# Router softmax of a tile split in three steps, its exponentials and normalization placed behind the previous tile's residual

## The reference, cut to what matters

```python
nx = layer_norm(x)
evidence = softmax(nx @ Wq @ k.T / 16) @ v
combined = concatenate([nx, evidence, anchor])
router_probs = softmax(combined @ router_W + router_b)           # [tokens, 3]
h = silu(einsum(combined, e_w1) + e_b1)                          # 3 experts x 512
routed = sum((einsum(h, e_w2) + e_b2) * router_probs, experts)
g = sigmoid(silu(combined @ gate_w1 + gate_b1) @ gate_w2 + gate_b2)
x1 = x + g * (routed @ out_w + out_b)
# second layer, on x1
q = (ada_ln(x1) @ Wq + bq)      # 16 heads of 16
out = x1 + softmax(q @ k.T / 4) @ v @ Wp + bp
```

## Time and profile before

| | |
|---|---|
| time, median of 3 runs | 438.69 us (437.05 to 439.32) |
| the profiled execution: its own time | 439.1 us |
| its span, from the first to the last instruction | 437.3 us |
| TensorE's mean granted clock | 0.988 of full speed |
| busy share of the span | PE 97%, PEld 88%, DVE 68%, ACT 51%, POOL 42% |
| chain that ended last, by engine | PE 75%, DVE 15%, DMA 3%, issue 3%, ACT 2% |

### The profile page before, as it was taken

The page is one execution under the profiler, slowest core; times in us unless marked ns, Lnnn a source line. Parts: engine busy times, 40 slices in busy tenths (PEclk is TensorE's granted clock), DMA queues, the critical chain, the costliest instruction groups (busy, mean ns, idle before and its releaser), DMA issues.

```text
span 437.3 us, 9617 instructions
## 1 busy us (share of the span) xinstructions
PE 422.5 (97%) x3613; PEld 383.6 (88%) x3613; DVE 297.5 (68%) x748; ACT 223.9 (51%) x487; POOL 185.1 (42%) x192
## 2 busy tenths in 40 slices
PE   7999999999999999999999999999999899979995
PEld 6578999999998899989998899889988897868875
DVE  2685475683776497739963897389558865982696
ACT  2777643345347633863467246724763466317271
POOL 3545573553453346323633454346343732341020
PEclk9699999999999999999999999999999999998999
DMA  9678001640200221024000400030003021200301
GB/s 285 229 269 323 23 28 31 164 96 19 56 4 2 55 67 28 25 56 138 1 5 13 109 1 5 16 84 0 5 22 77 0 54 35 73 4 25 72 3 49
DMA packets 16982, 27.94 MB, mean 64 GB/s; under 512 B 3816, under 2 KB 9256, under 8 KB 16808
## 3 DMA queue, kind: packets, MB, share of 16 engines
q1 hardware_dynamic: 16808, 27.32, 21.4%
q10 hardware_dynamic: 128, 0.01, 0.0%
HBM read 16.07 MB, written 2.10 MB: 42 GB/s over the span
## 4 chain that ended last, share of the span: by engine, by line
PE 75%; DVE 15%; DMA 3%; issue 3%; ACT 2%; SPq 1%; ACTq 0%
PE hidden_banks L1704 7%; PE hidden_banks L1705 7%; PE hidden_banks L1706 7%; PE score_banks L1711 5%; PE score_banks L2076 5%; PE token_bank L1704 5%; PE token_bank L1705 5%; PE token_bank L1706 5%; PE score_banks L2046 4%; PE value_bank L2099 3%; PE value_bank L2102 3%; PE value_bank L1711 3%; DVE head_maxima L1468 3%; PE hidden_banks L1929 2%; DMA unit_weights<-units 2%
## 5 line engine op out<-in xcount | busy, mean ns | idle before, releaser
L1627 POOL TENSOR_TENSOR hidden_low<-hidden,hidden_high 128x512 fp32r<-128x512 f32 x56 | 72.8, 1300 | 113.7 <-ACT hidden_high L1075 113.6
L1468 DVE TENSOR_REDUCE head_maxima<-score_banks 128x2 f32<-128x308 f32 x128 | 54.6, 474 | 16.6 <-PE score_banks L2046 14.4
L1704 PE MATMUL hidden_banks<-normed_high,hidden_w_high 128*128 128x256 f32 x224 | 64.2, 287 | 0.8 <-issue 0.8
L1705 PE MATMUL hidden_banks<-normed_high,hidden_w_low 128*128 128x256 f32 x224 | 62.5, 279 | 0.0
L1706 PE MATMUL hidden_banks<-normed_low,hidden_w_high 128*128 128x256 f32 x224 | 62.4, 279 | 0.0
L1137 ACT ACTIVATE exp_ring<-score_banks 128x512 f32<-128x512 f32 x96 | 52.6, 600 | 18.8 <-PE score_banks L2076 17.8
L1075 ACT CAST hidden_high<-hidden 128x512 fp32r<-128x512 f32 x56 | 34.9, 622 | 47.8 <-DVE hidden L1385 46.8
L1704 PE MATMUL token_bank<-expert_out_high,hidden_high 128*128 128x256 f32 x192 | 55.6, 289 | 0.0
L1067 ACT ACTIVATE hidden<-hidden_banks 128x512 f32<-128x512 f32 x56 | 33.4, 596 | 40.4 <-PE hidden_banks L1929 38.8
L1706 PE MATMUL token_bank<-expert_out_low,hidden_high 128*128 128x256 f32 x192 | 53.4, 278 | 0.0
L1705 PE MATMUL token_bank<-expert_out_high,hidden_low 128*128 128x256 f32 x192 | 53.4, 278 | 0.0
(11 more groups left out here) (289 smaller groups left out, 1119.7 us busy)
## 6 DMA issues: line engine op xcount, KB each, us to landing
unit_weights<-units SPq DMA_DIRECT2D x7, 768.0 KB, 6.4
query_stack<-queries_high SPq DMA_DIRECT2D x56, 64.0 KB, 2.0
tokens<-x SPq DMA_DIRECT2D x8, 256.0 KB, 3.8
query_stack<-queries_low SPq DMA_DIRECT2D x28, 64.0 KB, 2.0
w_slice<-units SPq DMA_DIRECT2D x7, 256.0 KB, 2.9
out<-tokens SPq DMA_DIRECT2D x7, 256.0 KB, 2.4
w_T<-folds SPq DMA_DIRECT2D x6, 256.0 KB, 6.1
pair_keys<-keys_high SPq DMA_DIRECT2D x16, 77.0 KB
```

What stands on the lines that cost most here:

```text
L1468: v.tensor_reduce(MX[:, s, first:first + step + 1:step], S[:, ring_of[key][0], 0:2 * CTX].rearrange("p (j n) -> p j n", j=2), AX.X, ALU.ma ...
L1627: nc.gpsimd.tensor_tensor(SL[:, ring(t, u), :], TB[:, ring(t, u), :], raw(SH[:, ring(t, u), :]), ALU.subtract).then_inc(gpsimd_h, 1)
L1704: mm(out_, lh, rh, start=start, stop=False, skip_group_check=skip)
L1705: mm(out_, ll, rh, start=False, stop=False, skip_group_check=skip)
```

## The change

The step `logit` is cut in three. `logit` keeps the two additions. `top` is the maximum, on DVE. `soft` is the two exponentials on ACT, and the reciprocal and the two scalings on DVE. Each has a slot of its own: `top` at 17, just ahead of `res` of the tile before (17.4); `soft` at 18.6, behind `shift` (18.5), with -0.8 on ACT where the exponentials had +1.7 to a slot of 14.4. Tile 0 is placed by the table of the setup. No instruction is added or dropped and none changes its operands; line numbers grow by 2 to 10.

```diff
-    "ln": 0.2, "norm": 1.6, "low": 6.6, "att": 7.9, "prob": 9.1, "route": 12.3, "logit": 14.4, "res": 17.4,
+    "ln": 0.2, "norm": 1.6, "low": 6.6, "att": 7.9, "prob": 9.1, "route": 12.3, "logit": 14.4, "top": 17, "soft": 18.6, "res": 17.4,
...
-        "logit": 1.7, "z": 0.81, "h": 0.3, "gate": 0.4, "qx": 0.4, "query": 0.1, "row": -0.4, "score": 0.2,
+        "soft": -0.8, "z": 0.81, "h": 0.3, "gate": 0.4, "qx": 0.4, "query": 0.1, "row": -0.4, "score": 0.2,
...
                 v.tensor_tensor(LG[:, :, :], LG[:, :, :], parts_of[:, 0, :, 0:EXPERTS], ALU.add).then_inc(vector_logit, 1)
-                dve.wait_ge(vector_logit, upto(vector_logit, key, "l"))
-                v.tensor_reduce(RT[:, 0, :], LG[:, :, :], AX.X, ALU.max, negate=True).then_inc(vector_logit, 1)
-                dve.wait_ge(scalar_logit, upto(scalar_logit, key, "ex"))
+
+            def top(key):
+                t = key[1]
+                dve.wait_ge(vector_logit, upto(vector_logit, ("logit", t), "l"))
+                if t:
+                    dve.wait_ge(scalar_soft, upto(scalar_soft, ("soft", t - 1), "ex"))
+                v.tensor_reduce(RT[:, 0, :], LG[:, :, :], AX.X, ALU.max, negate=True).then_inc(vector_top, 1)
+
+            def soft(key):
+                t = key[1]
+                dve.wait_ge(scalar_soft, upto(scalar_soft, key, "ex"))
                 v.reciprocal(RT[:, 2, :], RT[:, 1, :]).then_inc(vector_results, results.one())
                 dve.wait_ge(vector_results, results.n)
                 for s in range(NSUB):
                     last = v.tensor_scalar(PR[:, t % 2, s, :], PR[:, t % 2, s, :], RT[:, 2, s:s + 1], None, ALU.mult)
-                last.then_inc(vector_logit, 1)
+                last.then_inc(vector_soft, 1)
...
-                dve.wait_ge(vector_logit, upto(vector_logit, ("logit", t), "prob"))
+                dve.wait_ge(vector_soft, upto(vector_soft, ("soft", t), "prob"))
```

More of the change, by code:

```diff
@@ L180 @@
         "route": ["pm", "pd"],
-        "logit": ["ex"],
+        "soft": ["ex"],
         "z": ["t"],
@@ L210 @@
         "route": ["pl", "dl"],
-        "logit": ["l", "s", "prob"],
+        "logit": ["l"],
+        "top": ["s"],
+        "soft": ["prob"],
         "z": ["s"],
@@ L318 @@
     "unit": (0.99, 2.23, 3.75, 4.08, 9.23, 9.4, 9.94), "w2": (7.4, 10.3, 11.1, 13, 14.2, 17.9), "norm": -0.3,
-    "low": 1.7, "att": 2, "prob": 2.8, "route": 3.8, "logit": 4.75, "cb": 4.3, "bq": 12.2, "split": (8.74, 13.12),
+    "low": 1.7, "att": 2, "prob": 2.8, "route": 3.8, "logit": 4.75, "top": 6.4, "soft": 7.25, "cb": 4.3, "bq": 12.2, "split": (8.74, 13.12),
     "keyn": (11.4, 12.5), "keyx": (12.4, 13.8), "key": (13.4, 17.8), "mod": (9.2, 9.6, 10.3, 10.6), "ck": 10.8,
@@ L352, in schedule @@
         place(SETUP["vt"][u], ("vt", u))
-    for name in ("norm", "low", "att", "prob", "route", "logit"):
+    for name in ("norm", "low", "att", "prob", "route", "logit", "top", "soft"):
         place(SETUP[name], (name, 0))
@@ L384, in schedule @@
         if t:
-            for name in ("ln", "norm", "low", "att", "prob", "route", "logit"):
+            for name in ("ln", "norm", "low", "att", "prob", "route", "logit", "top", "soft"):
                 place(at - LOOP + plan(t, name), (name, t))
@@ L660, in build @@
          scalar_silu, scalar_split, scalar_keyx, scalar_bias2, scalar_norm, scalar_low, scalar_att,
-         scalar_route, scalar_logit, scalar_z, scalar_h, scalar_gate, scalar_xhat, scalar_qx, scalar_query,
+         scalar_route, scalar_soft, scalar_z, scalar_h, scalar_gate, scalar_xhat, scalar_qx, scalar_query,
          scalar_row, scalar_score, scalar_raw, scalar_out) = (
@@ L665, in build @@
          vector_group, vector_mod, vector_bq, vector_keyn, vector_key, vector_ln, vector_att, vector_prob,
-         vector_route, vector_logit, vector_z, vector_init, vector_evac, vector_res, vector_qn, vector_qlow,
+         vector_route, vector_logit, vector_top, vector_soft, vector_z, vector_init, vector_evac, vector_res, vector_qn, vector_qlow,
          vector_query, vector_most, vector_row, vector_dup, vector_sums, vector_out, vector_outl, vector_proj,
@@ L1046, in route @@
                 nc.scalar.copy(PTD[0:STACK, t % 2, :], H[0:STACK, TILE:2 * TILE]).then_inc(scalar_route, 1)
-            def logit(key):
+            def soft(key):
                 t = key[1]
-                act.wait_ge(vector_logit, upto(vector_logit, key, "s"))
+                act.wait_ge(vector_top, upto(vector_top, ("top", t), "s"))
                 for s in range(NSUB):
@@ L1053, in logit @@
                                                 accum_out=RT[:, 1, s:s + 1])
-                last.then_inc(scalar_logit, 1)
+                last.then_inc(scalar_soft, 1)
             def hidden(key):
@@ L1155, in _ @@
             parts = {"setup": setup, "silu": silu, "cv": context_v, "ck": context_k, "fold": fold, "gsplit": gate_split, "unit": unit, "vw": context_w, "vt": context_tail,
-                     "w2": w2, "split": split, "bias2": expert_bias, "keyx": keyx, "norm": norm, "low": low, "att": att, "route": route, "logit": logit,
+                     "w2": w2, "split": split, "bias2": expert_bias, "keyx": keyx, "norm": norm, "low": low, "att": att, "route": route, "soft": soft,
                      "z": hidden, "h": high, "gate": gate, "xhat": x_hat, "qx": qx, "query": query, "row": row,
@@ L1528, in _ @@
                      "vw": context_w, "vt": context_tail, "w2": w2, "cb": bias_out, "mod": mod, "bq": query_bias, "keyn": keyn, "key": pair_keys, "ln": ln,
-                     "att": att, "prob": prob, "route": route, "logit": logit, "z": hidden, "init": init, "evac": evac,
+                     "att": att, "prob": prob, "route": route, "logit": logit, "top": top, "soft": soft, "z": hidden, "init": init, "evac": evac,
                      "res": res, "qn": qn, "shift": shift, "qlow": qlow, "query": query, "most": most, "row": row, "dup": dup, "outl": outs_low, "sums": sums,
```

## The result

The changed kernel takes 439.61 us in the median of 22 runs (438.17 to 441.62), the kernel before 437.55 us in 22 runs beside them (436.05 to 440.18). The ratio is 1.0046, with a 95% interval of 1.0031 to 1.0060: 2.0 us slower (1.4 to 2.6). Forecast were 1.9 us more.

The account below looks back on a forecast made before the run. PE, busy for 97% of the span, was taken as the bound. Stalls of 1.83 us plus 0.1 us in tile 1 gave +1.9 us, or 440.6 us on the 438.69 us median; range 438.3 to 442.3 us.

Parts of the forecast that it names:

- What the broken-up wait is worth: Removing DVE's 5.9 us and ACT's 9.4 us of waits between maximum and exponentials over eight tiles gains PE nothing.
- Exponentials on ACT behind `h(t, 1)`: First three scores start 0.2 us late, made up before the third slice: price 0; without cover 0.2 to 0.67 us a tile.
- The DVE tail: Reciprocal and two scalings (0.57 us) plus a 0.04 us handover, behind the shift, delay the third hidden product by 0.61 us.
- Three stalls: PE's value group waits 0.61 us longer for score 5's exponential in tiles 2, 4 and 5: +1.83 us.
- Tile 3: The later exponential still meets PE's value group with about 0.1 us to spare: 0.
- Tiles 6 and 7: Biases stand behind the third product, which waits for ACT's tanh, so the scalings fall into idle time: 0.
- Tile 1: PE's wait for `x_hat`, with the earlier residual meeting POOL's `hidden_low`: +0.1 us, from -0.16 to +0.45.
- Tile 0: In the setup, where PE has other work: 0, at most +0.4 us if the scalings meet POOL.
- (b): Loss in tiles 2, 4 and 5 is hidden and only tile 1's is left: 438.8 us, chance 0.13.
- (d): Delay also reaches PE in tile 3 and one more tile, five times 0.61 us: 441.8 us, chance 0.16.
- (e): Scalings in their new place wait for a running POOL instruction, 1.07 us more in three tiles: 443.8 us, chance 0.04.
- Rival (c): `x_hat` of tile 0 starts early enough to end PE's 0.58 us wait, without stalls: 438.1 us, chance 0.07.

Follow-up runs that it names:

- e1: Changed kernel, with DVE's reciprocal and scalings in tiles 2 to 7 moved ahead of the shift, ACT's order kept; 0.9978 of the kernel before.
- e2: Changed kernel, with DVE's reciprocal and scalings moved ahead of the shift in tiles 3, 6 and 7 only; 1.0037 of the kernel before.
- e3: Changed kernel, with DVE's reciprocal and scalings moved ahead of the shift in tiles 2, 4 and 5 only; 0.9989 of the kernel before.
- e5: Changed kernel, with ACT's rounding of the third hidden slice put behind score 5's exponential in tiles 2 to 5; 0.9976 of the kernel before.
- e4: Changed kernel, with the reciprocal made four times instead of once in tiles 2 to 5; 1.0068 of the kernel before.
- e11: The kernel before, unchanged, run once more for its trace; 256.09 us from PE's first router matmul in tile 1 to that in tile 7.
- e10: The changed kernel, unedited, run once more for its trace; 257.85 us from PE's first router matmul in tile 1 to that in tile 7.
- e7: Changed kernel, with ACT taking x_hat of tile 0 ahead of tile 1's router exponentials, DVE's order kept; one execution, 439.15 us.

## Why the prediction was right

- **What the broken-up wait is worth: nothing.** Right. DVE's idle time ahead of the second product grew from 1.69 to 2.99 us, the forecast "near 3".
- **Exponentials on ACT behind `h(t, 1)`: 0.** Right, and shown by e1, which keeps them there without a loss.
- **The DVE tail: 0.61 us.** Measured 0.64 (228.87 to 229.51): the handover to the biases takes 0.09 us (229.42 to 229.51), where I had taken 0.04. The third product slips by 0.60 against the shift (3.09 - 2.49), since the reciprocal starts 0.04 us sooner behind the shift than L1400 did.
- **Three stalls, +1.83 us.** Right in place and size. Against the kernel before, PE's value group slips by 0.65, 0.59 and 0.59 us in tiles 2, 4 and 5, 1.83 in all; e1 takes 0.66, 0.61 and 0.60 back. e2 and e3 confirm the three tiles, e5 the path.
- **Tile 3, 0 with 0.1 us to spare.** Right; e4 used the margin up. Tiles 6 and 7: right, by e3.
- **Tile 1, +0.1 in a range of -0.16 to +0.45.** Measured +0.28: inside the range, nearly three times the term, and by another pair of instructions. I had the second half of the residual (L1434) hold up POOL's `hidden_low`, which in fact takes 1.27 us, against 1.28 before. What is lengthened is POOL's second `x_hat` instruction ahead of it, from 1.23 to 1.73 us, and `hidden_low` starts that much later. Both halves of the residual lie inside it; which of them lengthens it, no run separates:

```profile
92.63 1.73 POOL L1648 TENSOR_SCALAR x_hat<-tokens,mean_var,rstd 128x256 f32<-128x256 f32 x1
92.70 0.73 DVE L1441 SCALAR_TENSOR_TENSOR expert_sum<-gate,expert_sum 128x512 f32<-128x512 f32 x1
93.46 0.77 DVE L1444 TENSOR_TENSOR tokens<-expert_sum,tokens 128x512 f32<-128x512 f32 x1
```

The Trainium skill ("SBUF — State Buffer", who interferes with whom) has it that whoever issues first keeps the other out. The trace agrees that the two hold each other up, by 0.50 us, but not with the order: by the recorded starts POOL's instruction was first, by 0.07 us, and it was the one lengthened, while DVE's two took 0.73 and 0.77 us in place of 0.68 and 0.69.
- **Tile 0, 0.** Nothing against it: with the clock at full speed up to there, the stage begins at 89.44 us in the kernel before (e11) and at 89.49 in the change (e10). That is no finer than 0.3 us, since the two traces of e1 begin it at 89.85 and 89.53.
- **The sum.** That the stage shows just the forecast +1.93 us is in part luck: tile 1 cost 0.18 us more than its term, and the wait for the queries, which the forecast didn't have, came out 0.16 us shorter than before.
- **Rivals (b), (d) and (e)** didn't come: the three stalls are there, tile 3 has none, and in tiles 2 to 7 the two scalings take 0.36 us behind the shift, with POOL idle.
- **Rival (c)**, `x_hat` early enough to end PE's wait, needed ACT's order changed, as its counter-argument said; e7 did that and won 0.4 us.

## What to carry to other kernels

A wait between two engines costs nothing while a longer wait stands behind it on both, so its total in a table of waits is no price: here 15 us of such waits were removed and the kernel got 2 us slower. Work that leaves a place with idle time should go to another place with idle time, and the timeline shows it in brackets: the same instructions 0.15 slots earlier, in the 0.82 us of waiting for rstd, cost nothing. And where an engine's fixed order puts a late item ahead of an urgent one (the rounding ahead of score 5), exchanging the two cuts the path whatever the late item's delay.

## What the runs showed of the hardware that I had not expected

**Which POOL instructions hold up DVE.** The scalings (0.36 us for two) wait for POOL's `hidden_low`: one took 1.3 us in the earlier trace rows. In e1 they lie wholly inside POOL's rstd, from 226.00 to 226.71, which is a POOL instruction with two inputs too, on 128x2 elements,

```profile
226.00 0.71 POOL L1553 TENSOR_TENSOR rstd<-mean_var,minus_half 128x2 f32<-128x2 f32 x1
```

and still take 0.36 us. The residual of tile 1 likewise ran inside POOL's `x_hat` at nearly its usual length (above). So the recorded duration of a POOL instruction isn't the time for which it keeps DVE out. What the difference is, size or operation, no run here separates.

**The queries' transfer at tile 4.** Of the 84 such transfers in a trace SP issues all but two or three in 0.5 to 0.65 us each. One between 111 and 115 us takes 0.7 to 1.9 us in every one of the thirteen traces, and one at tile 4, between 237 and 243 us, 1.1 to 1.8 us. PE waits for this second one. In the change, then in e1:

```profile
240.76 0.59 SPq L875 DMA_DIRECT2D query_stack<-queries_low  x1
241.40 1.09 SPq L875 DMA_DIRECT2D query_stack<-queries_high  x1
```

```profile
238.12 0.59 SPq L877 DMA_DIRECT2D query_stack<-queries_low  x1
238.75 2.39 SPq L877 DMA_DIRECT2D query_stack<-queries_high  x2
```

In e1 the first of the two merged issues takes 1.75 us. PE waits 0.3 us in the change and 1.0 in e1, in two traces of each; SP's order is the same in both. It hid 0.7 us of what e1 wins over the change. In twelve of the thirteen traces PE's wait is the length of this issue less 0.8 us (in e3 less 0.4).

The DMA view of e1 from 238.6 to 240.6 us, queues with their packets, MB and share of 16 engines, shows what else is under way:

```profile
q1 hardware_dynamic: 94, 0.13, 28.9%
q8 instruction: 1, 0.02, 4.5%
```

One packet of 16 KB on the queue named instruction is in flight. In all thirteen traces such a packet is in flight during the long issue at tile 4, for 0.9 to 1.5 us, and the issue ends 0.2 to 0.4 us behind the packet's end; the same holds for the long one between 111 and 115 us. That the packet stretches the issue is argued from this coincidence and not shown: no run moved it. Why the packet takes longer in some kernels than in others stays open too.
